# Extra rows of the first mixture as quarter rows, turned by one transpose, and second-layer products in alternating order

## The reference, cut to what matters

```python
logits = xf @ router                                  # 8 experts
top_v, top_i = jax.lax.top_k(logits, 2)
w = jax.nn.softmax(top_v, axis=-1)
gates = jnp.sum(jax.nn.one_hot(top_i, E) * w[..., None], axis=1)
for e in range(E):
    h = xf @ W1[e]                                    # 512 -> 2048
    h = h * jax.nn.sigmoid(h)
    out = out + gates[:, e:e + 1] * (h @ W2[e])       # 2048 -> 512
```

## Time and profile before

| | us |
|---|---|
| median of 3 runs | 1708.62 |
| lowest, highest | 1704.49, 1716.28 |
| span of the profiled execution | 1710.0 |
| TensorE matmuls busy in it | 1608.9 |
| VectorE, ScalarE busy in it | 1028.7, 522.1 |

### The profile page before, as it was taken

One profiled execution on the slowest core, in us unless ns is written; L12 is line 12 of the kernel. 1 busy time (PEld: TensorE's weight loads), 2 busy tenths in 40 slices (PEclk: granted clock), 3 DMA queues, 4 the chain that ended last, 5 costly groups with the idle time before them and its releaser, 6 DMA issues. The chain is left out here.

```text
span 1710.0 us, 27863 instructions
## 1 busy us (share of the span) xinstructions
PE 1608.9 (94%) x9460; PEld 758.6 (44%) x9471; DVE 1028.7 (60%) x1681; ACT 522.1 (31%) x781; POOL 100.3 (6%) x82
## 2 busy tenths in 40 slices
PE   7999999999899889999999899998999899989997
PEld 3333333222343376666665433332222244467775
DVE  6677777999746551111111599998979945652223
ACT  3434434878413310000000211114658612200000
POOL 0200001000002010000000320000300001010001
PEclk9899998999999989999999999998999999989999
DMA  4442332211067967666661423210412021239996
GB/s 167 149 151 110 143 141 82 64 51 37 0 133 124 197 235 256 235 233 225 235 235 57 152 91 117 74 67 32 158 39 74 0 86 32 100 122 336 325 327 228
DMA packets 73420, 240.28 MB, mean 141 GB/s; under 512 B 7328, under 2 KB 20528, under 8 KB 54032
## 3 DMA queue, kind: packets, MB, share of 16 engines
q1 hardware_dynamic: 64752, 220.42, 39.8%
q10 hardware_dynamic: 6048, 10.69, 1.7%
q0 software_dynamic: 2560, 8.39, 1.5%
HBM read 214.04 MB, written 35.91 MB: 146 GB/s over the span
## 5 line engine op out<-in xcount | busy, mean ns | idle before, releaser
L1564 ACT ACTIVATE BIG<-banks 128x1024 f32<-128x1024 f32 (+5 forms) x320 | 282.1, 934 | 122.5 <-PE banks L1510 121.7
L1086 DVE CUSTOM_DVE_ANT_0 BIG<-banks,MASK,MX 128x512 bf16<-128x512 f32 (+5 forms) x384 | 228.9, 656 | 61.8 <-issue 38.3
L2106 PEld LDWEIGHTS banks<-KF,BIG 128*128 128x128 f32 x1792 | 227.0, 191 | 14.1 <-issue 14.1
L2106 PE MATMUL banks<-KF,BIG 128*128 128x160 f32 (+1 forms) x1792 | 229.2, 289 | 2.6 <-DVE KF L1824 2.0
L2134 PE MATMUL banks<-BIG,PB 128*128 128x512 f32 x448 | 202.9, 600 | 0.0
L695 PE MATMUL banks<-KF,XN 32*128 32x512 f32 (+4 forms) x1280 | 188.8, 609 | 11.4 <-DVE MX L1086 3.8
L1503 PE MATMUL banks<-XN,KF 32*128 32x512 f32 (+4 forms) x1280 | 187.9, 614 | 7.4 <-ACT BIG L1564 5.3
L1615 DVE TENSOR_TENSOR PB<-PB,BIG 128x2048 f32<-128x2048 f32 (+5 forms) x78 | 165.7, 2124 | 22.6 <-ACT BIG L1564 20.2
L1079 DVE TENSOR_REDUCE MXW<-banks 128x2 f32<-128x1024 f32 x128 | 150.3, 1216 | 44.6 <-PE banks L706 43.4
L1470 PE MATMUL banks<-BIG,V 128*32 128x512 f32 (+4 forms) x1280 | 160.4, 570 | 5.0 <-issue 2.6
L2134 PEld LDWEIGHTS banks<-BIG,PB 128*128 128x128 f32 x448 | 81.5, 190 | 113.1 <-issue 112.9
(11 more groups left out here) (296 smaller groups left out, 1468.1 us busy)
## 6 DMA issues: line engine op xcount, KB each, us to landing
BIG<-in_L0f_w SPq DMA_DIRECT2D x64, 1024.0 KB, 4.8
BIG<-in_L1f_w SPq DMA_DIRECT2D x48, 1024.0 KB, 5.7
BIG<-in_mask_q SPq DMA_DIRECT2D x16, 1024.0 KB, 8.0
k_saved<-KF SPq DMA_DIRECT2D x32, 256.0 KB, 2.7
CT<-in_ctx SPq DMA_DIRECT2D x6, 1024.0 KB, 4.8
XNT<-in_ctx SPq DMA_DIRECT2D x6, 1024.0 KB, 6.4
v_saved<-V SPq DMA_DIRECT2D x24, 256.0 KB, 2.4
KF<-k_saved SPq DMA_DIRECT2D x24, 256.0 KB, 3.3
```

The costliest lines, as they stand in the source:

```text
L1086: last = v.tensor_tensor_reduce(m.JUNK[:, 2 * half + e, k0:k1], pair[:, e, k0:k1], bias, 1.0, mx, ALU.add, ALU.max, mx)
L1564: a.activation(m.PE_[:, s % NP, 2 * half:2 * half + 2, q0:q1], m.pair[(2 * s + half) % 3][:, :, q0:q1], ACT.Exp).then_inc(exp_ready, 1)
L2106: last = t.matmul(out, W1[k][:, d, f * P:(f + 1) * P], XE[:, d, :], start=d == 0, stop=d == DC - 1)
```

## The change

The extra rows of a round are loaded as 128 quarter rows of 128 elements (row s, quarter c, at partition 4s + c), in place of 32 rows of 512. One 128x128 transpose turns them all, in place of four of 32x128. The transposed full rows land in one bank (4), the turned extra rows in another (5), and VectorE copies them out in two copies, the extra one with a stride. For round 0, whose rows come from the one-hot products, the old single copy stays, so there are two branches on `i`. In the second half of a round the extra products stand behind the full ones for even slices and ahead of them for odd ones. Where XTRA is 0 (the second mixture) no instruction of the extra rows is there; what changes for it is the place of the turned rows in PSUM and the branches on VectorE.

```diff
--- before.py
+++ after.py
@@ -1739,7 +1739,7 @@
 
     slot = [m.BIG[:, k * DC * KB:(k + 1) * DC * KB].rearrange("p (c n) -> p c n", c=DC) for k in range(8)]
     W1, W2 = slot[0:NF], slot[NF:2 * NF]
-    ROWS, ROWSX = m.CT[:, 0, :], m.CT[0:XTRA, 1, :]
+    ROWS, ROWSX = m.CT[:, 0, :], m.CT[:, 1, 0:P]
     XE = m.KF[:, :, :].rearrange("p c n -> p (c n)")[:, 0:DC * RS].rearrange("p (c n) -> p c n", n=RS)
     EX = m.V[:, :, :].rearrange("p c n -> p (c n)")[:, 0:8 * RS].rearrange("p (a b n) -> p a b n", a=2, b=2)
     HS = m.PB[:, :, :, :].rearrange("p a b n -> p (a b n)")[:, 0:4 * NF * RS].rearrange("p (a n) -> p a n", n=RS)
@@ -1750,6 +1750,8 @@
     KSRC, NEXT = m.MASK[:, 0], (0, 1, 6, 7)
     hidden = [m.pair[j][:, :, 0:2 * RS] for j in range(2)]
     tokens = m.pair[2][:, :, 0:2 * RS]
+    turned = m.pair[2][:, 0, :].rearrange("p (c n) -> p c n", c=DC)
+    turned_extra = m.pair[2][:, 1, 0:P]
     YB, YXB = m.bank[6], m.bank[7]
     slots = (NR + 1) * RS
     XS, YS = (t[0:slots, :].rearrange("(r s) d -> r s d", s=RS) for t in (m.XS, m.YS))
@@ -1892,9 +1894,16 @@
                             dve.wait_ge(activated, i * NF + k + 1 + B)
                             v.tensor_tensor(out, ex, hidden[k % 2], ALU.mult).then_inc(hidden_copied, 1)
 
-                    with dve.If(i + 1 < nr):
-                        wait_alone(dve, transposed, i + 2 + B)
-                        v.tensor_copy(XE[:, :, :].rearrange("p (a c) n -> p a (c n)", a=2), tokens).then_inc(tokens_copied, 1)
+                    with dve.If(i < 1):
+                        with dve.If(i + 1 < nr):
+                            wait_alone(dve, transposed, i + 2 + B)
+                            v.tensor_copy(XE[:, :, :].rearrange("p (a c) n -> p a (c n)", a=2), tokens).then_inc(tokens_copied, 1)
+                    with dve.If(i >= 1):
+                        with dve.If(i + 1 < nr):
+                            wait_alone(dve, transposed, i + 2 + B)
+                            if XTRA:
+                                v.tensor_copy(XE[:, :, P:RS], turned_extra.rearrange("p (s c) -> p c s", c=DC))
+                            v.tensor_copy(XE[:, :, 0:P], turned).then_inc(tokens_copied, 1)
                     if result is not None:
                         with dve.If(i < 1):
                             shares_of_last()
@@ -2009,7 +2018,8 @@
                         wait_alone(act, transposed, i + 2 + B)
                         act.dma_start(ROWS, XS[bass.ds(at + 2, 1), 0:P, :].rearrange("a s d -> (a s) d")).then_inc(rows_loaded, 16)
                         if XTRA:
-                            act.dma_start(ROWSX, XS[bass.ds(at + 2, 1), P:RS, :].rearrange("a s d -> (a s) d")).then_inc(rows_loaded, 16)
+                            act.dma_start(ROWSX,
+                                          XS[bass.ds(at + 2, 1), P:RS, :].rearrange("a s (c n) -> (a s c) n", c=DC)).then_inc(rows_loaded, 16)
                     if result is not None:
                         with act.If(i + 1 >= nr):
                             act.wait_ge(shares_turned, 1)
@@ -2084,10 +2094,9 @@
 
                 pe.wait_ge(rows_loaded, (i - 1) * (32 if XTRA else 16) + B)
                 for d in range(DC):
-                    out = tokens[:, d // 2, (d % 2) * RS:(d % 2) * RS + RS]
-                    last = t.transpose(out[:, 0:P], ROWS[:, d * P:(d + 1) * P], m.ident[:, :])
-                    if XTRA:
-                        last = t.transpose(out[:, P:RS], ROWSX[:, d * P:(d + 1) * P], m.ident[0:XTRA, 0:XTRA])
+                    last = t.transpose(turned[:, d, :], ROWS[:, d * P:(d + 1) * P], m.ident[:, :])
+                if XTRA:
+                    last = t.transpose(turned_extra, ROWSX, m.ident[:, :])
                 last.then_inc(transposed, 1)
 
             pe.wait_ge(steps_done, m.mark["counted"])
@@ -2121,18 +2130,25 @@
                     pe.wait_ge(output_copied, i + B)
                     if XTRA:
                         pe.wait_ge(extra_output_copied, i + B)
+                    def extra_products(k):
+
+                        for f in range(4):
+                            last = t.matmul(YXB[rows(f), :], HS[:, 4 * k + f, P:RS], W2[k][:, f, :],
+                                            start=k == 0, stop=k == NF - 1, skip_group_check=True)
+                        if k == NF - 1:
+                            last.then_inc(extra_ready, 1)
+                        return last
+
                     for k in range(NF):
                         pe.wait_ge(w2_loaded[k], i * 16 + 16 + B)
                         pe.wait_ge(hidden_copied, i * NF + k + 1 + B)
-                        if XTRA:
-                            for f in range(4):
-                                last = t.matmul(YXB[rows(f), :], HS[:, 4 * k + f, P:RS], W2[k][:, f, :],
-                                                start=k == 0, stop=k == NF - 1, skip_group_check=True)
-                            if k == NF - 1:
-                                last.then_inc(extra_ready, 1)
+                        if XTRA and k % 2:
+                            extra_products(k)
                         for f in range(4):
                             last = t.matmul(YB, HS[:, 4 * k + f, 0:P], W2[k][:, f, :],
                                             start=k + f == 0, stop=(k == NF - 1 and f == 3), skip_group_check=True)
+                        if XTRA and k % 2 == 0:
+                            last = extra_products(k)
                         last.then_inc(w2_used[k], 1)
                     if result is not None:
                         with pe.If(i + 1 >= nr):
```

## The result

| | before | changed |
|---|---|---|
| median, us | 1709.48 (12 runs) | 1700.52 (12 runs) |
| lowest, highest | 1703.18, 1716.28 | 1690.77, 1706.42 |
| ratio of the runs | | 0.9944, 95% interval 0.9925 to 0.9964 |
| span of the profiled execution | 1710.0 | 1689.0 |

The change makes the kernel 0.56% faster: 1709.5 x 0.0056 = 9.6 us, with an interval of 6 to 13 us; the medians lie 9.0 us apart. The forecast was 10.8 us less and 1697.8 us.

A forecast was written before the change was run, and what follows sets the result against it. TensorE's own stream was taken to bound the first mixture's rounds. Transposes (6 x 1.13) plus order (4.0) gave 10.8 us less: 1699.2 for the profiled span, 1697.8 us for the median, range 1690.5 to 1705.

The forecast's parts named there:

- The bound: First mixture's rounds: TensorE is busy 38.6 of 38.6 us at clock 1.00, so only its own stream's savings count.
- The cost of a change of form: Full blocks between extras in the first mixture: 3.63 us instead of 3.43, so 0.20 us for the two changes around them.
- Part 1: Alternating order of extra and full second-layer products: 0.48 us less a round, 4.0 us in all, bounds 2.6 to 4.8.
- Part 2: Five 128x128 transposes replacing eight of two forms: 1.13 us less in each of six rounds, 6.8 us.
- Parts 3 and 4: Transfer of extra rows as 128 packets, and VectorE's two copies plus branches: both hidden, cost 0.
- The sum: Whole kernel: 6 x 1.13 + 4.0 = 10.8 us less, median 1697.8 us, 0.63% less.
- Rival (a): Extra pairs don't chain; loads of added waves show, order gains only 0.06 us a round: 1701.1 us, chance 0.09.
- Rival (b): Saving right, but half-clock stretches after the first mixture shift by 6.7 us: 1704.5 or 1691.1 us, chance 0.12.
- Rival (c): VectorE's loop body outgrows what it holds, code fetched every round, second mixture waits: 1740 us, chance 0.02.

The follow-up runs named there:

- e4_one_run: The changed kernel with all sixteen extra products in one run ahead of the last slice's full block: round 36.61 us against 36.95, ratio 0.9914 against the kernel before.
- e3_grouped: The kernel before with its eight transposes sorted, four 128x128 first, then four 32x128: round 37.86 us against 38.65, whole time 1705.33 us, taken once.
- e6_wide_fold: e4_one_run with the fold's stationary tile widened from 32 to 128 columns: round 36.30 us against 36.61, ratio 0.9911 against the kernel before.

## Why the prediction was right

- **The bound.** TensorE busy for the whole round at clock 1.00, so a saving in its stream is a saving in the time: shown. In every experiment the round became shorter by what TensorE's own instructions took less, and when nothing covered VectorE's copy, the wait of 0.81 us came out in the round.
- **The cost of a change of form.** 0.20 us for a full block between extras, read from durations of two mixtures. Shown by e4_one_run (one block of extras fewer between full ones), e3_grouped (same instructions, sorted) and e6_wide_fold (same work, another form). But 0.20 is only the part that shows on the full block. An excursion into another form and back costs 0.34 us in all (36.95 - 36.61), the rest lying on the extra block, which takes 1.00 us where two waves at 0.429 would take 0.86. The forecast was not hurt by this, since it added up whole measured blocks. The Trainium skill's rule (TensorEngine Tiling (Array Packing), Key Properties) that changing the mode drains TensorE agrees with all of them: no change of form here was free.
- **Part 1, order.** Forecast 0.48 us a round and 0.09 in the first and last round, 4.0 in all. Measured 1.86 for a pair of extra blocks in place of 1.90: added waves follow at 0.429, not 0.45, since only the first spacing behind a change is longer (1.00 us for two waves, 1.86 for four, 3.57 for eight). That was my upper bound: 0.58 a round. In round 0 the order gave 0.67. With eight rounds 4.8 us in place of 4.0. This is the one term that was mis-sized.
- **Part 2, transposes.** Forecast 1.13 us in each of six rounds, measured 1.14 (1.68 less 0.54): 6.8 us.
- **Parts 3 and 4** cost nothing in the rounds. The strided copy took 0.28 us, between my bounds of 0.1 and 0.8. That the packets don't show held: both loads of rows land 0.8 us later, but they do so in e3_grouped too, with the old packets. The forecast had not seen that shorter transposes bring them closer to the 1 MB load ahead. It stayed hidden.
- **The sum.** 6.8 + 4.8 = 11.6 us in the mixture, forecast 10.8, measured on the whole 9.6 with an interval from 6 to 13. Whole times can't tell 10.8 from 11.6; that the mechanism was right is known from the rounds alone. How near the median came (1700.5 for 1697.8) is partly luck: the forecast started from a median of three runs that lay 0.9 us below that of twelve, and the saving in the rounds was larger than forecast while that in the medians was smaller.
- **Rival (a)**, the loads of the added waves show, would have made a pair 2.11 us; it took 1.86. The rule on overlapping weight loads (the Trainium skill, TensorE: Matmul & The Clock Gate, Part 3) is not borne out for column tiles: eight waves follow at the cadence of full passes.
- **Rival (b)**, stretches at half clock, did not set the medians but goes with the scatter. Ahead of the mixture it made 11 us between the two profiled executions, and of the twelve runs of the changed kernel the one with the lowest granted clock (0.970) took 1706.42 us and the one of 1690.77 had 0.978, the highest. Not all of the scatter is the clock: the second round of the second mixture varies as well.
- **Rival (c)**, code fetched in every round, did not come: from the third on, the rounds of the second mixture stayed at 14.45 us (the first took 17.68 us before and 17.69 after), and VectorE has no wait put down to "remote" there. What the prediction set against it, a single packet of code in the first mixture, should have read two, both in round 0.

## What to carry to other kernels

Where TensorE is the bound, sort its instructions by tile form, and count the borders: in this kernel each excursion into another form and back cost 0.26 us (a small transpose between large ones: 0.79 us for three), 0.31 (the fold) or 0.34 (the extras), whatever work lay between. Leave one long block behind the group whose result another engine must copy before TensorE goes on; the order with the fewest borders lost because nothing covered that copy. Judge such a change by the length of a repeated round in the trace, which holds to 0.01 us, and not by whole times, which scatter by 10 us and more with the clock of other stretches.

## What the runs showed of the hardware that I had not expected

- A run of 32x128 transposes goes at 0.06 us each, while 128x128 ones go at 0.109; between changes of form each pair of them took 0.43 us.
- Waves of four column tiles follow at 0.429 us, the cadence of full 512-column passes, however many; only the first one behind a change of form is followed after 0.45.
- A stationary tile of 128 columns made the fold 0.12 us shorter than one of 32, because it kept the neighbours' form.
- A load's time to landing went with how closely it followed another load: the 256 KB load took 4.0 us when issued 1.61 us behind a 1 MB load on another queue, 4.7 at 0.81 (both with 32 packets of 2 KB behind it) and 4.8 at 0.57 (with 128 of 512 B).
